# A six-layer float32 kernel: the seam between the experts and the second layer, the order of the last tiles, and the layout of one copy

## The reference, cut to what matters

```python
x = x + xattn0(layernorm(x), ctx)          # gated by gelu(x k) * (x k)
x = x + attn0(layernorm(x))                # causal, 16 heads, rotary
x = x + moe(layernorm(x))                  # 32 experts, 2 per row
x = x + xattn1(layernorm(x), ctx)          # 16 heads, softmax over 257 keys
x = attn1(x)                               # group norm, linear attention, group norm, silu feed-forward
x = x + real(ifft(fft(layernorm(x)) @ w)) + bias
```

## Time and profile before

| | us |
|---|---|
| median of 3 runs | 2104.41 (2103.45 to 2105.27) |
| the profiled execution | 2104.48 |
| its span | 2102.9 |
| TensorE busy | 1949.2 (93%) |
| VectorE, ScalarE, GpSimd busy | 695.9, 541.3, 195.2 |
| DMA | 374.96 MB, mean 178 GB/s |

### The profile page before, as it was taken

The page is one execution under the profiler, slowest core; times in us unless marked ns, Lnnn a source line. Parts: engine busy times, 40 slices in busy tenths (PEclk is TensorE's granted clock), DMA queues, the critical chain, the costliest instruction groups (busy, mean ns, idle before and its releaser), DMA issues.

```text
span 2102.9 us, 37580 instructions
## 1 busy us (share of the span) xinstructions
PE 1949.2 (93%) x15760; PEld 999.2 (48%) x15760; DVE 695.9 (33%) x1500; ACT 541.3 (26%) x1113; POOL 195.2 (9%) x182
## 2 busy tenths in 40 slices
PE   5888887999999999999995999999999999999968
PEld 2444464333333333333333656566665656575535
DVE  2666551121111211112124233433334333334233
ACT  1333211222222222222111223232323323232221
POOL 1122203000000000000003000000000000000010
PEclk9999999999999999999997999999999999999989
DMA  9544137999999999999975200000000000000000
GB/s 342 210 161 160 60 127 274 391 396 385 381 378 371 378 357 377 374 376 377 359 294 174 98 21 22 27 21 17 21 22 26 21 27 11 26 21 26 11 1 10
DMA packets 86296, 374.96 MB, mean 178 GB/s; under 512 B 7782, under 2 KB 25702, under 8 KB 53432
## 3 DMA queue, kind: packets, MB, share of 16 engines
q1 hardware_dynamic: 79544, 355.71, 44.3%
q0 software_dynamic: 6656, 17.77, 2.3%
HBM read 357.73 MB, written 16.45 MB: 178 GB/s over the span
## 4 chain that ended last, share of the span: by engine, by line
PE 69%; issue 17%; DVE 5%; POOL 4%; ACT 2%; DMA 2%; SPq 1%; POOLq 0%; DVEq 0%; ACTq 0%
PE ps L1242 25%; PE ps L1420 16%; PE ps L1402 16%; POOL arena L534 4%; PE ps L1410 3%; PE ps L1621 2%; PE ps L1428 1%; DMA arena<-in_wproj0T 1%; PE ps L1544 1%; ACT arena L704 1%; PE ps L1302 1%; PE ps L1391 1%; PE ps L1332 1%; PE ps L1502 1%; PE ps L1518 1%
## 5 line engine op out<-in xcount | busy, mean ns | idle before, releaser
L1242 PE MATMUL ps<-arena 128*128 128x257 f32 (+3 forms) x3208 | 908.7, 440 | 44.8 <-ACT arena L793 17.9
L1242 PEld LDWEIGHTS ps<-arena 128*128 128x128 f32 x3208 | 546.7, 194 | 372.3 <-issue 290.5
L1420 PE MATMUL ps<-arena 128*32 128x512 f32 x3072 | 373.6, 594 | 0.0
L1402 PE MATMUL ps<-arena 128*32 128x512 f32 x3072 | 362.5, 594 | 0.6 <-issue 0.6
L534 POOL TENSOR_TENSOR arena<-arena 128x1 f32<-128x1 f32 (+3 forms) x80 | 128.2, 1602 | 1121.8 <-DVE arena L875 612.8
L1059 DVE COPY arena<-ps 128x512 f32<-128x512 f32 x96 | 66.3, 691 | 485.6 <-PE ps L1420 485.6
L1402 PEld LDWEIGHTS ps<-arena 128*32 128x32 f32 x3072 | 107.4, 109 | 226.6 <-issue 226.4
L1420 PEld LDWEIGHTS ps<-arena 128*32 128x32 f32 x3072 | 99.2, 109 | 197.6 <-issue 191.5
L754 ACT ACTIVATE arena<-ps 128x512 f32<-128x512 f32 x96 | 57.3, 597 | 354.7 <-PE ps L1402 354.7
L1150 DVE TENSOR_REDUCE arena<-ps 128x1 f32<-128x257 f32 x128 | 54.1, 423 | 163.8 <-PE ps L1502 163.8
L783 ACT ACTIVATE arena<-ps,arena 128x257 f32<-128x257 f32 x128 | 60.6, 476 | 148.4 <-PE ps L1242 148.4
(11 more groups left out here) (194 smaller groups left out, 1314.3 us busy)
## 6 DMA issues: line engine op xcount, KB each, us to landing
arena<-in_w SPq DMA_DIRECT2D x64, 4096.0 KB, 13.7
arena<-in_ctxT SPq DMA_DIRECT2D x8, 2056.0 KB, 7.9
arena<-in_ctxT SPq DMA_DIRECT2D x32, 514.0 KB, 3.7
arena<-in_ctx SPq DMA_DIRECT2D x8, 2048.0 KB
xe_rows<-arena SPq DMA_DIRECT2D x8, 616.0 KB
arena<-in_b POOLq DMA_DIRECT2D x32, 154.0 KB, 7.4
arena<-xe_rows SPq DMA_DIRECT2D x32, 154.0 KB
y_rows<-arena POOLq DMA_DIRECT2D x32, 154.0 KB, 6.2
```

The costliest lines, as they stand in the source:

```text
L1242: ins = pe.matmul(dst, lhsT, rhs, start=(n == 0), stop=(n == len(pairs) - 1))
L1402: ins = pe.matmul(ps[q4[n], t, :], xeT[s][:, k, q4[t]], w1_sb[s][:, k, n * D:(n + 1) * D], start=(k == 0), stop=(k == KD - 1))
L1420: ins = pe.matmul(ps[q4[n], ST + t, :], hT[s][:, t, c, q4[n]], w2_sb[s][:, n * HB + c, :], start=(c == 0), stop=(c == HB - 1))
```

## The change

1. `hidden_out` writes `h_sb` in the order that `turned` needs: ScalarE reads PSUM in steps of four elements, TensorE's transposes read dense chunks.
2. At the seam: TensorE runs the first half of batch 0's keys ahead of the last fold, then the other half and both value products of batch 0. The context of batches 0 and 1 and `bv` are loaded ahead of wqkv1T and owT, and WvT, WqT and bv have a semaphore of their own. GpSimd gathers tile 0, does its normalization's root, and only then issues the other 14 gathers. `clast` and `vlast` follow `head(0)`. VectorE's additions of tiles 1 to 7 are pieces of `PLAN_C` beside tile 0's cross. fw1T and fw2T are loaded after tile 0.
3. `tail` has 16 pieces (each feed-forward product in two halves), and `PLAN_Y` and `PLAN_Z` are new.
4. `bv_sb` and one of the `hT` buffers have other places in memory.

```diff
-        h0, xe0, xe1, h1 = W.take(ST, HB, HB * T), W.take(D), W.take(D), W.take(ST, HB, HB * T)
+        h0, xe0, xe1, _, h1 = (W.take(ST, HB, HB * T), W.take(D), W.take(D), W.take(2 * KD),
+                               W.take(ST, HB, HB * T))
...
-        WA, WK, WC, WF = 6, 3, 16, 2
+        WA, WK, WV, WC, WF = 6, 3, 3, 13, 2
...
         PLAN_C = ("ct" "cct" "cct" "cc"
                   "ct" "ccth" "ccth" "cth" "c"
+                  "ct" "cct" "cct" "ctt" "c"
+                  "ctt" "cct" "ccc" "ct")
+
+        PLAN_Y = ("ct" "cct" "cct" "cc"
                   "ct" "cct" "cct" "ct" "c"
-                  "ct" "cct" "ccc" "ct")
-
-        PLAN_Y = "ct" "cct" "cct" "cc" "ccccccc" "ccccccc" "ccccccc"
-
-        PLAN_Z = "tuttutuutuututututuututuu"
+                  "ct" "cct" "cct" "cc" "ccccccc")
+
+        PLAN_Z = "tutuuutuututut" "uuuuuuuu"
...
             run(head(0))
-            if after_head is not None:
-                after_head()
-            interleave(PLAN_C, c=cross(0, True), h=head(1))
+            beside = {} if after_head is None else after_head()
+            interleave(PLAN_C, c=cross(0, True), h=head(1), **beside)
...
-            load_c(wC_in, (WvT_sb, rows(WvT)), (WqT_sb, rows(WqT)), (WoT_sb, rows(WoT)))
+            load_c(wV_in, (WvT_sb, rows(WvT)), (WqT_sb, rows(WqT)))
+            load_c(wC_in, (WoT_sb, rows(WoT)))
             sp.wait_ge(y_ps, ST * (E - 1))
-            load_c(wC_in, (wqkv1_sb, rows(wqkv1T)), (ow_sb, rows(owT)))
...
             load_ctxc(0, 0)
+            load_c(wV_in, (bv_sb, bv.partition_broadcast(P)))
+            load_ctxc(1, 1)
+            load_c(wC_in, (wqkv1_sb, rows(wqkv1T)), (ow_sb, rows(owT)))
+            sp.wait_ge(y_ps, ST * E)
+            sp.dma_start(clast[0:B, :], ctx[:, S - 1:S, :].rearrange("b s d -> b (s d)")).then_inc(clast_in, 16)
             for s in range(2):
                 sp.wait_ge(y_stored[s], 16 * (E // 2))
-            sp.dma_start(clast[0:B, :], ctx[:, S - 1:S, :].rearrange("b s d -> b (s d)")).then_inc(clast_in, 16)
-            load_ctxc(1, 1)
-            load_c(wC_in, (bv_sb, bv.partition_broadcast(P)), (bo_sb, bo.partition_broadcast(P)),
+            load_c(wC_in, (bo_sb, bo.partition_broadcast(P)),
...
-            sp.wait_ge(moe_added, 2 * NT)
-            load_c(wF_in, (fw1_sb, rows(fw1T)), (fw2_sb, rows(fw2T)))
...
             tile_c(0, True)
+            sp.wait_ge(moe_added, 2 * NT)
+            load_c(wF_in, (fw1_sb, rows(fw1T)), (fw2_sb, rows(fw2T)))
...
+            gather(0)
...
+            def gather_others():
+                for i in range(1, NT):
+                    gather(i)
+                return {}
...
-                    act.activation(h_sb[:, t, :], ps[:, t, :], ACT.Copy).then_inc(h_out, 1)
+                    act.activation(h_sb[:, t, :].rearrange("p (c f) -> p c f", c=HB),
+                                   ps[:, t, :].rearrange("p (f c) -> p c f", c=HB), ACT.Copy).then_inc(h_out, 1)
...
             def head(i):
                 layer_norm(0, tile_of(x_sb, i), xn, NT + i, xn_rdy[0])
                 yield
+                if isinstance(i, int) and i == 0:
+                    values_out(0, 0, 0)
+                    values_out(0, 0, 1)
...
             def other_tiles():
-                queries()
+                yield
                 dve.wait_ge(gathered, 32 * (NT - 1))
                 for i in range(1, NT):
-                    add_experts(i)
+                    for k in range(2):
+                        add_expert(i, k)
+                        if (i, k) not in ((1, 0), (NT - 1, 1)):
+                            yield
                 dve.wait_ge(wC_in, 16 * WC)
+                yield
+
+            def first_tile():
+                queries()
+                dve.wait_ge(vlast_ps, 1)
+                TT(vlast_all[0:B, :], ps[0:B, 7, :], bv_sb[0:B, :], ALU.add).then_inc(vlast_rdy, 1)
+                return {"t": other_tiles()}
...
-                        ins = pe.transpose(ps[:, t, chunk(c)], h_sb[:, t, c:D:HB], id_sb)
+                        ins = pe.transpose(ps[:, t, chunk(c)], h_sb[:, t, chunk(c)], id_sb)
...
             pe.wait_ge(wK_in, 16 * WK)
-            run(keys(0, 0, None))
-            pe.wait_ge(clast_in, 16)
...
+            first_keys = keys(0, 0, None)
+            next(first_keys)
+            folded(E - 1)
+            run(first_keys)
+            pe.wait_ge(wV_in, 16 * WV)
+            for n in range(NV):
+                pe.wait_ge(k_ev, n + 1)
+                values(n, 0)
+            phase_c(pe, head, cross, tail, None, None, lasts)
```

More of the change, by code:

```diff
@@ L208, in perceiver_kernel @@
         ctxT_c = W.take(KD, 2 * S)
+        bv_sb = W.take(D)
         PTd = W.take(H, P)
-        bv_sb, bo_sb, ob_sb, fb2_sb, fbias_sb = (W.take(D) for _ in range(5))
+        bo_sb, ob_sb, fb2_sb, fbias_sb = (W.take(D) for _ in range(4))
         decay_sb = W.take(H, T)
@@ L257, in perceiver_kernel @@
         b1_ps = sem("b1_ps")
[L258 removed]
+        gathered, gathered0, moe_added, wK_in, wV_in, wF_in = (sem(n) for n in (
+            "gathered", "gathered0", "moe_added", "wK_in", "wV_in", "wF_in"))
         ctxc_in = [sem(f"ctxc_in{s}") for s in range(2)]
@@ L599, in _, with gather @@
                 pool.wait_ge(y_stored[s], 16 * (E // 2))
-            for i in range(NT):
+            def gather(i):
                 for k in range(2):
@@ L1097, in _ @@
             dve.wait_ge(y_ps, ST * E)
-            for s in range(2):
-                dve.wait_ge(y_stored[s], 16 * (E // 2))
             step(dve.memset(one.PTd, 0.0))
@@ L1491, in keys, with values @@
                         yield
+            def values(n, s):
+                group(ps[:, bV(n), :],
+                      [(ctxT_c[:, k, s * S + n * P:s * S + (n + 1) * P], WvT_sb[:, k, :]) for k in range(KD)], v_ps)
             def cross(i, more):
@@ L1509, in cross @@
                                 pe.matmul(ps[q4[q], bPV, :], zero_c[0:1, 0:DH], bv_sb[0:1, :], start=True, stop=False)
-                        pe.wait_ge(exp_c, HG * bb + (n + 1))
-                        group(ps[:, bV(n), :],
-                              [(ctxT_c[:, k, s * S + n * P:s * S + (n + 1) * P], WvT_sb[:, k, :]) for k in range(KD)],
-                              v_ps)
+                        if not opening:
+                            pe.wait_ge(exp_c, HG * bb + (n + 1))
+                            values(n, s)
                         yield
@@ L1628, in tail, with lasts @@
                 yield
-            pe.wait_ge(wK_in, 16 * WK)
-            run(keys(0, 0, None))
-            pe.wait_ge(clast_in, 16)
-            for k in range(KD):
-                ins = pe.transpose(ps[:, 5, k * B:(k + 1) * B], clast[0:B, chunk(k)], id_sb[0:B, 0:B])
-            ins.then_inc(clT_ps, 1)
-            pe.wait_ge(wC_in, 16 * WC)
-            pe.wait_ge(clT_rdy, 1)
-            pe.wait_ge(y_rdy, E)
-            group(ps[0:B, 6, :], [(clastT[:, k, :], WvT_sb[:, k, :]) for k in range(KD)], vlast_ps)
-            phase_c(pe, head, cross, tail, None, None)
+            def lasts():
+                pe.wait_ge(clast_in, 16)
+                for k in range(KD):
+                    ins = pe.transpose(ps[:, 5, k * B:(k + 1) * B], clast[0:B, chunk(k)], id_sb[0:B, 0:B])
+                ins.then_inc(clT_ps, 1)
+                pe.wait_ge(clT_rdy, 1)
+                group(ps[0:B, 7, :], [(clastT[:, k, :], WvT_sb[:, k, :]) for k in range(KD)], vlast_ps)
+                return {}
+            pe.wait_ge(wK_in, 16 * WK)
+            first_keys = keys(0, 0, None)
[7 more added lines that the diff above has]
+            phase_c(pe, head, cross, tail, None, None, lasts)
 def constants():
```

52 lines of the change are left out of this document (35 added, 17 removed).

## The result

The changed kernel takes **2096.63 us** (median of 7 runs, 2095.99 to 2097.08) against 2105.05 for the kernel before in the same session (2101.64 to 2106.09): ratio 0.996, 95% interval 0.995 to 0.997. It is faster by 8.4 us, 0.4%. I had predicted 2077.7 and a range of 2066 to 2090; the direction was right, the gain is a third of what I said, and the time lies outside the range.

A forecast was written before the change was run, and what follows sets the result against it. The prediction took TensorE to bound the expert phase, with DMA close behind, and saw TensorE often waiting in the seam. 2104.5 - 10.6 - 21.0 + 4.8 = 2077.7 us, range 2066 to 2090.

The forecast's parts named there:

- Part 1: Expert phase: TensorE's 12 transposes per expert read dense chunks, 0.33 us less in each of 32 experts, -10.6 us.
- 110 ns each: Transposes in the expert phase: price of a dense one, against 137.5 ns with steps of four elements.
- ScalarE's read at no cost: Expert phase: ScalarE's PSUM read in steps may get slower, but 8 us of cover hide it; costed at nothing.
- rival 1: Expert phase: the step costs nothing and the dense transposes gain nothing; 2088.3 us in total, chance 6%.
- Part 2: Seam between experts and second layer: new order brings the second batch's scores to 1151.5 against 1172.50, -21.0 us.
- What could be late next: Seam: 14 gathers land by 1145 to 1148, VectorE needs them before the second softmax; cover of 1 to 4 us.
- The fold behind the first keys: Seam: the last fold, now after the first half of the keys, shifts everything through the gather 2.6 us later.
- Part 3: End, tiles 6 and 7: TensorE's work unchanged, its waits grow from 27.1 to 31.9 us, +4.8 us.
- I book nothing: End: two to three low-clock stretches, each -0 to +2 us, priced at zero; bounds -4 to +9 us.
- Rival 2: Seam gives less: 14 gathers land late, VectorE stands before the second softmax; 2079 to 2084 us, chance 16%.
- Rivals 3, 4 and 5: End a gain, 2068, 12%; granted clock low through last tile, 2110, 3%; early keys wait as before, 2089, 3%.
- three signs that the forecast named for being wrong: Transposes keep 1.65 us; VectorE waits for gathers with TensorE behind it; waits after the loop sum under 25 us.

The follow-up runs named there:

- old end: The changed kernel with its end undone (old plans C, Y, Z, unsplit feed-forward pieces; layout and seam as changed): 2086.41 us, ratio 0.9908 to the kernel before.
- The fills: The changed kernel with 20 unused matmuls (5, 6, 4 and 5) in TensorE's waits at its end: 2088.40 us, ratio 0.9912 to the kernel before.

## Why the prediction was wrong, step by step

- **Part 1, -10.6, measured -5.7.** The mechanism was right (weight loads 212 to 140 ns), the size wrong. I took 137.5 ns against 110, both as time per transpose up to the next kind. But the 12 entries of the earlier trace rows last 1.72 us with 0.28 for the last: 0.131 us from one to the next, and (1.53 - 0.27) / 11 = 0.115 after. The step that failed is "110 ns each" as the price of a dense transpose here: the dense ones come every 0.115 us, and about 0.08 us between the last transpose and the next matmuls is there before and after, so the layout doesn't touch it. 1.65 less 1.46 in each of the 32 experts is 6.0 us. ScalarE's read at no cost: right. The rule of steps that are free up to 4 fp32 elements of the Trainium skill ("SBUF — State Buffer", Door 1: The DMA port swizzle) doesn't hold for these loads: 140 against 212 ns, so rival 1 was rightly low. What the Trainium skill says there of PSUM is about matmuls; the prediction stretched it to ScalarE's read, which kept its 0.60 us.
- **Part 2, -21.0, measured -12.7 (old end: -12.5).** Right: no wait before the keys, the additions 15.8 us after the last result (forecast 14.9), the first query matmul at 21.8 (20.3), the softmax in 4.3. Wrong: everything beside the 14 gathers. The queries are taken up at 29.2 us where 25.3 was forecast, the `vlast` addition starts at 37.0 (30.7), the softmax at 39.2 (31.6). The step that failed is "What could be late next": I named the 14 gathers and looked only at who waits for their data. Their cost is what they do to TensorE while in flight. Taking that away gave 6.2 to 6.4 of the 8.3 us, and the first softmax then starts 31.8 us after the last result, on the forecast's 31.6. The other 2 lie behind it, at the lower clock: 1.76 us from the transposes to the keys where I took 0.9, and 9.03 from there to the products where I took 8.0.
- **The fold behind the first keys, +2.6:** it cost 1 at most, since with the fold first the store is issued 2.7 us earlier and lands only 0.1 earlier. Why, no run shows.
- **Part 3, +4.8, measured +8.9 (alone +10.2).** The waits were right, 31.8 against 31.9, one for one: 2.54, 5.06, 3.66, 5.79, 4.67. That they add 4.8 was right too: 31.8 less 27.1 is 4.7. The step that failed is "I book nothing" for the clock, which is the other 4.2. The kernel before had two such stretches, as the prediction said, and they cost 1.6 (15.59 for 14.0) and 2.2 us (12.95 for 10.75); it saw two to three in the change, and there are four, at 9.0 us together. Some came back, since the products that took 1.93 us before now take 1.08. The fills, which stand in the waits and keep the clock up, gave 8.2 us back. The prediction's own bounds for this part, -4 to +9, hold the 8.9.
- **Rivals.** Rival 2 (the seam gives less because of the 14 gathers) named the right instructions and the wrong victim: VectorE didn't stand waiting for their data before its second softmax. Rivals 3, 4 and 5 are out: the end was no gain, nor did the clock stay low throughout, and the early keys didn't wait.
- None of the three signs that the forecast named for being wrong came: the transposes did not keep their 1.65 us, VectorE didn't wait for gathers, and the waits sum to 31.8. A list of signs needs one for every term of the sum, and the clock and TensorE's ends beside the gathers had none.
- The range failed since it covered one part off at a time; all three were off to the same side. 5.2 in part 1, 8.3 in the seam, 4.1 at the end, 0.7 in the loop and 0.6 by which the kernel before measured slower beside the change (2105.05) than in the forecast (2104.5) make the 18.9 us.

## What to carry to other kernels

When a TensorE record and its consumer don't fit together, believe the consumer: look there for what else was in flight. Spread software gathers in bursts of few behind which TensorE has little to run, and price them by what they do to other engines, not only by when they land. Count what a wait of 4 to 6 us costs behind it, at the lower clock (here 1.6 to 2.5 us each time), and put spare matmuls into it when nothing useful fits, sized by their entries in the trace: twice too many made the kernel slower.

## What the runs showed of the hardware that I had not expected

- While 14 software gathers (issued by GpSimd) fly (17 to 21 us), TensorE's work is held up from 4 to 8 us after their first packet, 32 to 44 of its entries later. With the gathers behind the first softmax it came nearly to a stop: 3 or 4 entries in 2 us. With 4 (5.5 us) nothing is seen, with 8 (12.5 us), 2 to 3 us are lost. Hardware-queue traffic does nothing of the kind: not at 0.65 of the DMA engines' time (constants at 1111 to 1116 us of the change, with two gathers at 0.30 beside them), nor in the expert phase at 0.94. In the kernel before, TensorE had only 31 entries to run from the gathers' first packet to their landing, and no consumer was late.
- What exactly stops TensorE was not tried and stays open. My reading was the supply of its instructions, and a late block of them is not what the records show. The DMA records have one packet of 16 KB at a time on a queue of kind "instruction", which keeps step with TensorE's entries and so is likely its own. With the gathers behind the first softmax one stands at 1129.1 us and the next at 1157.2, and TensorE was at full speed again 1.1 us before the second. 180 entries lie between the two, and as many in the run with gathers in bursts, where nothing was held up (1128.1 and 1147.5 us).
- The effect travels with the gathers, so a faster TensorE in front of it wins little: with `vlast` early the queries took 3.84 instead of 5.96 us and were taken up 3.5 us earlier, and of that 1.4 us was left at the second scores.
- The exclusion of VectorE and GpSimd that the forecast weighed (the Trainium skill, "SBUF — State Buffer", SBUF: two separate sides) is small here: gathers issued beside VectorE's additions, which have two inputs in SBUF, took up to 1.27 us where others took 0.96, and three such additions took 2.32 us with gathers beside them (bursts) and without (the change). For two SBUF inputs the Trainium skill limits it there to GpSimd operations that read SBUF, which the prediction left out.
- Five unused matmuls in a wait of 5.1 us bring the 24 entries behind it from 13.02 to 10.57 us and the granted clock there from 0.71 to 1.00.
